# Second cross attention: fp32 keys in four row groups instead of bf16 parts, and queries made one head ahead

## The reference, cut to what matters

```python
def _L1_xattn_ref(x, y, mask, ...):            # x: layer norm of the tokens, y: ctx_1024
    q = (x @ Wq + bq).reshape(b, t, NUM_HEADS, HEAD_DIM)
    k = (y @ Wk + bk).reshape(b, kv_t, NUM_HEADS, HEAD_DIM)
    v = (y @ Wv + bv).reshape(b, kv_t, NUM_HEADS, HEAD_DIM)
    content = jnp.einsum('bthd,bThd->bhtT', q + r_w_bias, k)
    pe = _sinusoid_reversed(b, kv_t, DMODEL) @ Wp + bp
    rel = jnp.einsum('bthd,bThd->bhtT', q + r_r_bias, pe)
    rel = _relative_shift(rel)
    attn = (content + rel) * (1.0 / math.sqrt(HEAD_DIM))
    attn = attn * mask - 10000000000.0 * (1.0 - mask)
    p = jax.nn.softmax(attn, axis=-1)
    out = jnp.einsum('bhtT,bThd->bthd', p, v).reshape(b, t, DMODEL)
    return out @ Wo + bo
```

## Time and profile before

| | |
|---|---|
| time, median of 3 runs | 1509.57 us (1506.08 to 1513.34) |
| the profiled execution | 1510.08 us, span 1508.3 us |
| mean granted clock | 0.891 |
| busy: PE, PEld, DVE, ACT, POOL | 1146.1, 697.8, 975.6, 844.2, 546.8 us |
| DMA | 292.31 MB, mean 194 GB/s; 62.2% of 16 engines' span |
| `xb_kr<-key_rows` and `xb_kc<-key_rows` | 16 transfers each of 768 KB, 10.4 and 8.9 us to landing |
| `key_rows<-xa_parts`, the transfers with three copies | 16 of 768 KB, 3.5 us to landing |
| first rows of `cross1` | SP 744.04 (the load of Wq), ACT 744.05 (the load of its table for the root) |
| the loop over the units, first and last add (L2060) begins | 784.63, 1303.36 |

### The profile page before, as it was taken

One profiled execution on the slowest core, in us unless ns is written; L12 is line 12 of the kernel. 1 busy time (PEld: TensorE's weight loads), 2 busy tenths in 40 slices (PEclk: granted clock), 3 DMA queues, 4 the chain that ended last, 5 costly groups with the idle time before them and its releaser, 6 DMA issues. The chain is left out here.

```text
span 1508.3 us, 24545 instructions
## 1 busy us (share of the span) xinstructions
PE 1146.1 (76%) x7851; PEld 697.8 (46%) x7851; DVE 975.6 (65%) x1612; ACT 844.2 (56%) x1162; POOL 546.8 (36%) x213
## 2 busy tenths in 40 slices
PE   7677777729999868799736777777777777746798
PEld 3233333314434456688603444444444444424587
DVE  5898898950101465522338999999999999735321
ACT  3699999948898335233125555656556565313210
POOL 1256656620000040000016666667667676500000
PEclk9899999969999788899957889999999998757899
DMA  8876566447552420044669999999999998242040
GB/s 264 263 231 172 162 201 176 144 146 160 108 106 52 142 107 1 28 154 153 222 223 327 327 324 306 323 308 308 315 318 309 310 313 290 67 132 86 0 168 7
DMA packets 109176, 292.31 MB, mean 194 GB/s; under 512 B 11929, under 2 KB 46906, under 8 KB 94523
## 3 DMA queue, kind: packets, MB, share of 16 engines
q1 hardware_dynamic: 109120, 291.61, 62.2%
...
## 5 line engine op out<-in xcount | busy, mean ns | idle before, releaser
L2039 POOL TENSOR_TENSOR xb_row<-xb_row,w_mask 128x1024 f32<-128x1024 f32 x128 | 359.7, 2825 | 383.7 <-DVE xb_row L2060 383.6
L2069 DVE CUSTOM_DVE_ANT_0 xb_row<-xb_row,xb_minus 128x1024 f32<-128x1024 f32 x128 | 235.4, 1839 | 0.1
L2015 ACT COPY xb_turned<-xb_turn_ps 128x1024 f32<-128x1024 f32 x64 | 64.8, 1012 | 216.2 <-PE xb_turn_ps L1938 216.2
L2060 DVE TENSOR_TENSOR xb_row<-xb_cont_ps,xb_row 128x1024 f32<-128x1024 f32 x128 | 155.7, 1216 | 38.6 <-DMA xb_row<-rel_scores 23.9
L1938 PE MATMUL xb_turn_ps<-_ident,xb_row 128*128 128x128 f32 x1024 | 165.8, 315 | 15.7 <-ACT xb_turned L2015 15.5
L1938 PEld LDWEIGHTS xb_turn_ps<-_ident,xb_row 128*128 128x128 f32 x1024 | 142.2, 168 | 48.9 <-issue 47.6
L2004 ACT COPY xb_out<-xb_rel_ps 128x1024 f32<-128x1024 f32 x128 | 130.1, 1017 | 48.5 <-PE xb_rel_ps L1920 39.9
L573 DVE TENSOR_REDUCE xa_stats<-xa_b_ps 128x1 f32<-128x1024 f32 x128 | 152.9, 1217 | 3.9 <-PE xa_b_ps L472 3.6
L859 ACT ACTIVATE xa_probs<-xa_psT,xa_t_now 128x1024 f32<-128x1024 f32 x128 | 141.2, 1114 | 23.6 <-PE xa_psT L818 23.5
L522 ACT ACTIVATE xa_exps<-xa_b_ps,xa_stats 128x1024 f32<-128x1024 f32 x128 | 142.7, 1115 | 8.6 <-DVE xa_stats L573 6.2
L2009 ACT ACTIVATE xb_row<-xb_row,xb_ntop 128x2048 f32<-128x2048 f32 x64 | 128.9, 2014 | 0.5 <-DVE xb_ntop L2075 0.2
...
## 6 DMA issues: line engine op xcount, KB each, us to landing
xb_row<-rel_scores SPq DMA_DIRECT2D x128, 512.0 KB, 6.2
...
xb_kr<-key_rows SPq DMA_DIRECT2D x16, 768.0 KB, 10.4
...
```

The source lines that it names most:

```text
L2039: nc.gpsimd.tensor_tensor(row[:, u, at:at + SUB], row[:, u, at:at + SUB], mask[:, t, half * HALF + at:half * HALF + at + SUB], ALU.mult).t ...
L2060: nc.vector.tensor_tensor(row[:, u, at:at + SUB], cont_ps[:], row[:, u, at:at + SUB], ALU.add).then_inc(s["cont_out"], 1)
L2069: nc.vector.tensor_tensor_reduce(out=row[:, u, at:at + SUB], in0=row[:, u, at:at + SUB], in1=minus[:, t, half * HALF + at:half * HALF + at ...
```

## The change

It has two parts. The keys are stored once, in fp32, in `key_blocks`: block j holds the content keys of head j-1 and the relative keys of head j, each 16 rows, as eight pieces of 512 keys. POOL's splitting goes, and ACT waits for the stores (`keys_stored`) before it overwrites `whole`. Two transfers fill the unused halves of the first and the last block with finite numbers.

In `cross1`, SP loads one block of 512 KB a head in place of two loads of 768 KB; it lies on 4 groups of 32 rows, two pieces of 512 keys in each. A score is an fp32 matmul over 32 rows, of which the queries of the other kind are zero; part 0 uses row groups 0 and 1, part 1 uses 2 and 3. The queries come from the layer-normed tokens, a head ahead: ACT copies the next head's 32 columns of Wq four times side by side (`turn_weights`, once in four slots), PE multiplies (two fp32 matmuls of 256 columns, ahead of bring_together), and DVE adds the bias and scales twice (128x256 each). The parts of the queries, their store and their load are gone, and the two blocks have become one, with `minus` set behind the first queries.

```diff
-def store_key_parts(sp, dst, src, stored):
-
-
-    at = 0
-    for part, times in K_TIMES:
-        copies = src[:, part].unsqueeze(1).to_broadcast([P, times, QUARTER])
-        sp.dma_start(dst[:, at:at + times], copies).then_inc(stored, 16)
-        at += times
...
+def store_keys(sp, dst, src, stored):
+
+    for r in range(QUARTER // BANK):
+        sp.dma_start(dst[:, r], src[:, r * BANK:(r + 1) * BANK]).then_inc(stored, 16)
+
+
+def load_keys(f, sp, dst, block, loaded):
+
+    src = f.key_blocks[bass.ds(block, 1)].rearrange("j (a r) k d n -> (j r k d) a n", a=NHALF)
     sp.dma_start(dst, src).then_inc(loaded, 16)
...
+                finite = i["ctx_1024"][0:DK].rearrange("d (b n) -> b d n", n=BANK)
+                for block_at, kind in ((0, 0), (H, 1)):
+                    sp.dma_start(f.key_blocks[block_at, :, kind], finite).then_inc(s["edges_stored"], 16)
...
-                    sp.wait_ge(s["split_done"], HPB * it + c + 3)
-                    store_key_parts(sp, key_stores[1 + c // KC, c % KC][bass.ds(it, 1)].rearrange("g p c n -> p (g c) n"),
-                                    parts[:, b], parts_out[b])
                     sp.wait_ge(s["product_out"], NU // 2 * (HPB * it + c + 2))
+                    first_block = c % KC * (H // KC) + 1 - c // KC
+                    dst = by_quarter[c // KC][bass.ds(it, 1), first_block:first_block + H // KC]
+                    store_keys(sp, dst.rearrange("g j r d n -> (g j) r d n"), whole[:, b], keys_stored[b])
...
-                            act.wait_ge(s["split_done"], h + 1)
+                            act.wait_ge(keys_stored[c % 2], KEYS_OUT * (it * HPB // 2 + c // 2 + 1))
...
-                with pool.Fori(0, NB) as it:
-                    for c in range(HPB):
-                        split(it, c)
...
-                        load_keys(p, c + 2 * U, 2, kr96, kr_loaded)
-                    if c % U == 2 and (n is None or 0 <= n < UNITS - U):
-                        if n is None or n >= U:
-                            sp.wait_ge(s["cont_mm"], 2 * U * (2 * p + c // U))
-                        load_keys(p, c + U, 1, kc96, kc_loaded)
+                        load_keys(f, sp, kk[:, c // U % 2], 2 * p + c // U + 2, k_loaded[c // U % 2])
...
-                load_query_parts(f, sp, qc96, 1, q_loaded[0])
-                sp.dma_start(gather[:], i["c_gather"]).then_inc(g_loaded, 16)
+                small = ((wq[:], i["L1_xattn_Wq"]), (kinds[:], i["c_kinds"]), (qbias[:], i["L1_xattn_bq"]),
+                         (rbias[:], i["L1_xattn_r_bias"]), (gather[:], i["c_gather"]))
+                for dst, src in small:
+                    sp.dma_start(dst, src).then_inc(s["small_loaded"], 16)
+                for b in range(2):
+                    load_keys(f, sp, kk[:, b], b, k_loaded[b])
...
-                        at = half * HALF + part * SUB + k * BANK
-                        mm = nc.tensor.matmul(out[:, k * BANK:(k + 1) * BANK],
-                                              q96[0:ROWS, bass.ds(head, 1), t * P:(t + 1) * P],
-                                              k96[:, b, at:at + BANK], start=True, stop=True)
+                        r = part * (SUB // BANK) + k
+                        rows = slice(r * HEAD_PAIR, (r + 1) * HEAD_PAIR)
+                        mm = nc.tensor.matmul(out[:, k * BANK:(k + 1) * BANK], qq[rows, b, kind, t * P:(t + 1) * P],
+                                              kk[rows, b, half], start=True, stop=True)
                     mm.then_inc(done, 1)
...
+                def make_queries(p, c):
+
+                    block_at, b = 2 * p + c // U + 2, c // U % 2
+                    pe.wait_ge(s["w_turned"], block_at + 1)
+                    for k in range(KC):
+                        mm = nc.tensor.matmul(new_q, wturn[:, b, k, :], xnT[:, k, :], start=(k == 0), stop=(k == KC - 1))
+                    mm.then_inc(s["q_mm"], 1)
...
-                    if isinstance(n, int) and n == 0:
-                        pe.wait_ge(q_loaded[0], 96)
-                        pe.wait_ge(g_loaded, 16)
+                    if c % U == 0 and (n is None or n < UNITS):
+
+                        block_at = 2 * p + c // U + 1
+                        pe.wait_ge(s["q_made"], 2 * block_at + 2)
+                        pe.wait_ge(k_loaded[(c // U + 1) % 2], 16 * (p + (c // U + 1) // 2 + 1))
                     if runs(n, 0):
                         content(p, c, 0)
+                    if runs(n, -3):
+                        pe.wait_ge(s["sums_sb"], where(p, c - 3)[0] + 2)
+                    if makes_queries(n, c, 1):
+                        make_queries(p, c)
                     if runs(n, -3):
                         bring_together(p, c - 3)
...
+                    if makes_queries(n, c, 0):
+                        turn_weights(p, c)
+
+                def turn_weights(p, c):
+
+                    block_at, b = 2 * p + c // U + 2, c // U % 2
+                    if not (isinstance(n_of(p, c), int) and block_at < 2):
+                        act.wait_ge(s["q_mm"], block_at - 1)
+                    pair = wq[:, :, bass.ds(block_at * DK, HEAD_PAIR)].unsqueeze(2).to_broadcast([P, KC, NQ4, HEAD_PAIR])
+                    nc.scalar.copy(wturn[:, b].rearrange("p k (r n) -> p k r n", r=NQ4), pair).then_inc(s["w_turned"], 1)
+
+                n_of = lambda p, c: where(p, c)[0]
+                act.wait_ge(s["small_loaded"], 80)
+                turn_weights(0, -2 * U)
+                take_root(f, act, s["var_ready"], s["root_ready"])
+                act.wait_ge(s["xnT_mm"], 1)
+                nc.scalar.copy(xnT[:], xnT_ps).then_inc(s["xnT_sb"], 1)
...
+                    if makes_queries(n, c, 1):
+                        make_queries(p, c)
+
+                def make_queries(p, c):
+
+                    block_at, b = 2 * p + c // U + 2, c // U % 2
+                    dve.wait_ge(s["q_mm"], block_at + 1)
+                    for kind in range(2):
+                        nc.vector.tensor_scalar(qq[:, b, kind], new_q, qbias[:, bass.ds(block_at, 1)],
+                                                kinds[:, kind:kind + 1], ALU.add, ALU.mult).then_inc(s["q_made"], 1)
+
+                step = Chain(dve, s["dve_steps"])
+                layer_norm(f, dve, step, xn, f.x, 1e-5, s["var_ready"], s["root_ready"])
+                dve.sem_inc(s["xn_ready"], 1)
+                dve.wait_ge(s["small_loaded"], 80)
+                step(nc.vector.tensor_tensor(qbias[:], qbias[:], rbias[:], ALU.add))
+                make_queries(0, -2 * U)
+                for t in range(NT):
+                    nc.vector.tensor_scalar(minus[:, t], mask[:, t], 1.0, 1e10, ALU.subtract, ALU.mult
```

More of the change, by code:

```diff
@@ L1759, in _ @@
-            @block.tensor
-            def _(pe):
-                pe.wait_ge(s["xn_ready"], 1)
-                transpose_tokens(nc, tiles(0), xn, f.ident[:]).then_inc(s["xnT_mm"], 1)
-                pe.wait_ge(s["loaded"], 32)
-                pe.wait_ge(s["xnT_sb"], 1)
-                for m in range(KC):
-                    for c in range(KC):
-                        mm = nc.tensor.matmul(tiles(1)[:, m], wq[:, c, m * P:(m + 1) * P], xnT[:, c, :],
-                                              start=(c == 0), stop=(c == KC - 1))
-                mm.then_inc(s["q_mm"], 1)
@@ L1804, in cross1 @@
             s = {n: f.sem("b_" + n) for n in names}
+            k_loaded, v_loaded = ([f.sem(f"{n}_loaded{b}") for b in range(2)] for n in ("k", "v"))
             turned_sb = [f.sem(f"b_turned_sb{n}") for n in range(2)]
@@ L2541, in lay_out @@
         a[f"L1_xattn_{n}"] = np.asarray(v[f"L1_xattn_{n}"])
-    for n in ("bk", "bp", "bq", "bv"):
+    for n in ("bk", "bp", "bv"):
         a[f"L1_xattn_{n}"] = columns(v[f"L1_xattn_{n}"])
```

173 lines of the change are left out of this document (57 added, 116 removed).

## The result

The changed kernel takes 1522.86 us (median of 5 runs, 1520.61 to 1525.52) against 1509.57 before: ratio 1.0084, 95% interval 1.0063 to 1.0105. It is slower by 13.3 us between the medians (12.7 by the ratio), where 1512 was forecast with a range of 1487 to 1545. The profiled execution took 1520.61 us, its span is 1518.8.

A forecast was written before the change was run, and what follows sets the result against it. The prediction took the loop as bound by DVE and POOL handing over, 8.1 us a slot, and by PE where its clock is low. Terms: 1510.1 - 5 - 4.2 - 2 + 2.8 + 3.9 + 5.7 + 1 = 1512.3; range 1487 to 1545.

The forecast's parts named there:

- Pass b, -5: Pass b: without POOL's split, ACT's exponentials no longer wait for DVE's maxima; -5 us, bounds 0 and -6.2.
- its end, -4.2: End of pass b: last key stores issued earlier, no longer behind POOL, and one fewer; -4.2 us, range to -6.
- Prologue, -2: Start of cross1: first relative scores come earlier, but each part takes longer; -2 us, between 0 and -8.
- Row groups at once: Score matmuls: fp32 products over 32 rows in different row groups overlap, 0.88 us for a pair plus a tail.
- Changes between modes at nothing: PE switching between matmuls over 128 and over 32 rows: no gap seen, costed at nothing.
- The rival: PE's mode changes: each drains the engine, about 0.15 us apiece, giving 1518 us; chance 0.06.
- Main loop, full clock, +0.25 a query slot: Loop slots making queries at full clock: second add late, 0.25 us left; 11 slots, +2.8 us, bounds 0 and +8.
- Main loop, half clock, +10.6: Loop slots at half clock: longer score pairs +3.9, queries ahead +5.7, further cold slots +1 us.
- the clock holds: Loop and prologue: busier PE stays at full clock, half-clock terms and today's waits vanish; 1487 to 1501 us, chance 0.32.
- The clock falls: Loop: products over 32 rows get full clock less readily, more slots at half clock; 1562 us, half 1537, chance 0.2.
- Four groups do not overlap: Loop: content pairs must wait for relative pairs, making the second add late; 1540 us, chance 0.07.
- The transfers are the bound: Loop: DMA bounds it, so 16 MB less of keys saves 52 us; 1458 us, chance 0.03.

The follow-up runs named there:

- pool_load: Changed kernel with POOL's four split operations back in pass b, on tiles of their own that nobody waits for; 1527.09 us, one run.
- root_first: Changed kernel with ACT taking the layer norm's root before it waits for the small loads and copies the weights; 1519.06 us, ratio 1.0063.
- fill3: As fill6, but with three unused transposes per slot in place of six; 1496.93 us, ratio 0.9904.
- fill6: Changed kernel with root_first's move, query matmuls ahead of the xb_sumsT wait, and six unused transposes in slots without queries; 1493.04 us, ratio 0.9892.
- two_groups: Changed kernel with part 1 of all scores on row groups 0 and 1, so relative and content pairs cannot overlap; 1540.15 us, one run.
- before_fill6: Kernel before the change with six unused transposes in each loop slot, ahead of bring_together; 1504.33 us, ratio 0.9961.

## Why the prediction was right, and where it was off

The time fell into the range, and the sum of 1512.3 missed the profiled execution by 8.3. The range is 58 us wide, and the prediction had faster and slower nearly even (0.37 and 0.36), so it did not know the direction; it forecast 2.2 us of loss in the profiled execution, and 10.5 came. What was right is the mechanism of most steps, one by one:

- **Pass b, -5; its end, -4.2.** Measured -3.6 and -4.8. POOL's share in the waits is shown by pool_load. The step that was costed at nothing without a row is ACT's new wait for the keys' stores; it took 1.3, nearly all of the 1.4 that pass b missed. The time of pass b scatters, though: over the kernels with this change but pool_load, its last exponentials start from 306.6 to 310.5, against 311.7 and 312.0 before.
- **Prologue, -2.** Measured -1.2. The first relative scores were forecast 13.7 us after the stage's begin (12.4 measured), parts at 3.0 (3.18), and the add bound by PE, as it is. That ACT's weights stand ahead of the root was taken as the worst case; it was the case, and root_first shows its price, 3.7.
- **Row groups at once.** Right: 0.01 us between the starts of relative and content passes, a pair through in 1.12. TensorE: Matmul & The Clock Gate, Part 3, of the Trainium skill says that matmuls in different row groups run at once, and the trace agrees.
- **Changes between modes at nothing.** From the start of the eight transposes to the scores behind them it was 0.91 us before (1016.76 to 1017.67) and is 1.01 now (1014.37 to 1015.38), so the change from 128 rows to 32 costs at most 0.1 more than the one from 128 to 96 did; what that one costs no run shows. The rival had 0.15. At full clock, in slots without queries, nobody waits for it. TensorEngine Tiling (Array Packing), Key Properties, of the Trainium skill has each change of mode drain the engine; beyond this 0.1 the trace shows none of it.
- **Main loop, full clock, +0.25 a query slot.** Measured 8.36 against 8.11.
- **Main loop, half clock, +10.6.** This term was mis-sized. With the 2.8 of the query slots it was to be 13.4, and the loop lost 17.1. The step that failed is that 0.65 of each wait is lost. The rows say it otherwise: of a wait of 0.88, 0.57 was lost; of 1.34, 9.13 - 8.11 = 1.02; of 2.27, 10.06 - 8.11 = 1.95. Each time it is the wait less 0.31 or 0.32, and over all slots in which the second add alone waits over 0.35 the median difference is 0.33 before (18 slots, 0.29 to 0.44) and 0.32 now (25 slots, 0.27 to 0.45). The slack is a constant, so all that makes a late pair later is lost in full: 5 x 1.75 is 8.8, not 5.7, and 0.3 x 20 is 6.0, not 3.9. By places, the slots with queries grew by 11.2, where 2.8 + 5.7 and a quarter of the 3.9 make 9.5, and the others by 5.9, where 3.9 was forecast. The kernel before had the rows to see it: here a wait of 0.40 lost 933.80 - 925.61 - 8.11 = 0.08, a fifth of it.

```profile
925.61 1.21 DVE L2060 TENSOR_TENSOR xb_row<-xb_cont_ps,xb_row 128x1024 f32<-128x1024 f32 x1
...
928.91 1.22 DVE L2060 TENSOR_TENSOR xb_row<-xb_cont_ps,xb_row 128x1024 f32<-128x1024 f32 x1 [0.40 <-PE xb_cont_ps L1920]
...
933.80 1.21 DVE L2060 TENSOR_TENSOR xb_row<-xb_cont_ps,xb_row 128x1024 f32<-128x1024 f32 x1
```

- **Other layers.** 1.9 between pass b and `cross1` and 1.0 behind the loop are in unchanged code, and nothing was forecast there. The first stretch is 422.4 and 423.0 us in the two kernels with the old keys and 423.6 to 426.8 in all others, so some of it may be real; its cause is not shown. The 1.0 is less than the kernels differ there (200.8 to 206.0 us from the last unit's first add to the end, 211.5 in fill3).

The sum is 3.7 (loop) + 1.7 (starts) + 2.9 (other layers) = 8.3.

Of the rivals, "the clock holds" didn't come by itself: PE got busier and the clock only rose from 0.91 to 0.93. fill6 lies in its range (1487 to 1501, measured 1493), but only in part by its terms. The loop gave 7.1 where that rival had 5.8; of the 8 for the start 5.0 came, and 3.7 of these by the move of root_first, for the clock stayed at half up to the first add. "The clock falls" didn't come either; there were fewer slots with half-clock time (20 in place of 27), the ones in places 1 and 3 each dearer. "Four groups do not overlap" was made by hand: two_groups, 1540.15, for a forecast of 1540. That the numbers meet is luck: there the clock held in most of the loop, and 14 us come from its one fall; it is a single run. "The transfers are the bound": with the clock held the changed loop took 511.6 and the old one 513.1 us with a DMA share of 0.96 (before_fill6; 0.82 in fill6), so the traffic was worth nothing that can be told.

What stays open: why the clock falls in one slot and not in the next. The runs show what pushes it (idle time, filling over 32 rows in place of 128, four groups at once in place of two pairs in a row) and not by which measure.
